# The norms' reciprocal square roots in a Flamingo-style stack on one core: a power on GpSimd in place of Newton rounds on VectorE

## What is computed

```python
def _layernorm(x, axis=-1, eps=1e-05):
    m = jnp.mean(x, axis=axis, keepdims=True)
    v = jnp.var(x, axis=axis, keepdims=True)
    return (x - m) / jnp.sqrt(v + eps)

x = x + jnp.tanh(g_xattn[0]) * _L0_xattn_ref(_layernorm(x), ctx, ...)   # differential attention
x = x + jnp.tanh(g_ffn[0])   * _L0_ffn_ref(_layernorm(x), ...)          # three coupled rotations
x = x + jnp.tanh(g_xattn[1]) * _L1_xattn_ref(ctx, _layernorm(x), mask, ...)
x = x + jnp.tanh(g_ffn[1])   * _L1_ffn_ref(_layernorm(x), ...)          # 2 shared + 8 routed experts
x = x + jnp.tanh(g_xattn[2]) * _L2_xattn_ref(_layernorm(x), ctx, ctx, ...)
x = x + jnp.tanh(g_ffn[2])   * _L2_ffn_ref(_layernorm(x), ...)          # attention, then 8 experts
x = x + jnp.tanh(g_xattn[3]) * _L3_xattn_ref(_layernorm(x), ctx, ctx, ...)
x = x + jnp.tanh(g_ffn[3])   * _L3_ffn_ref(_layernorm(x), ...)
```

```python
def layernorm(x, g, b):
    mu = jnp.mean(x, axis=-1, keepdims=True)
    var = jnp.var(x, axis=-1, keepdims=True)
    return (x - mu) * jax.lax.rsqrt(var + EPS) * g + b
```

## Time and profile before

| What | Value |
|---|---|
| Runs | 5879.70, 5902.63, 5884.03 us |
| Median | 5884.03 us |
| Span of the profiled execution | 5884.8 us |
| TensorE busy | 4971.8 us, 84% |
| VectorE busy | 3010.4 us, 51% |
| ScalarE busy | 1835.7 us, 31% |
| POOL busy | 404.4 us, 7% |
| Mean granted TensorE clock | 0.908 |

### The profile page before, as it was taken

The page is one execution under the profiler, slowest core; times in us unless marked ns, Lnnn a source line. Parts: engine busy times, 40 slices in busy tenths (PEclk is TensorE's granted clock), DMA queues, the critical chain, the costliest instruction groups (busy, mean ns, idle before and its releaser), DMA issues.

```text
span 5884.8 us, 74338 instructions
## 1 busy us (share of the span) xinstructions
PE 4971.8 (84%) x29184; PEld 3568.6 (61%) x29184; DVE 3010.4 (51%) x7402; ACT 1835.7 (31%) x3060; POOL 404.4 (7%) x244
## 2 busy tenths in 40 slices
PE   6998789987899878998789887798877988789887
PEld 4565755657556575565755657556675566655666
DVE  5445554455444555445554555535555355553555
ACT  3324143241432414224142241422424224142231
POOL 0000200001000020001100011000110001100011
PEclk8998889988799888998889999899998999989898
DMA  2000100001000010000100001000000000000000
GB/s 92 1 28 8 36 25 1 28 8 36 25 1 28 6 38 25 1 28 8 36 25 1 28 8 36 25 1 28 15 29 25 1 28 15 33 22 1 28 15 33
DMA packets 34483, 126.67 MB, mean 22 GB/s; under 512 B 3136, under 2 KB 15424, under 8 KB 25664
## 3 DMA queue, kind: packets, MB, share of 16 engines
q1 hardware_dynamic: 34112, 121.62, 6.0%
HBM read 117.41 MB, written 4.19 MB: 21 GB/s over the span
## 4 chain that ended last, share of the span: by engine, by line
PE 65%; DVE 24%; ACT 5%; issue 4%; DMA 1%; SPq 0%; POOL 0%; DVEq 0%; ACTq 0%
PE w L409 15%; PE w L419 9%; DVE mx L1006 7%; PE o L550 6%; PE w L666 5%; DVE oth_lo L1294 5%; PE w L508 4%; PE w L522 4%; PE w L399 4%; PE w L658 4%; PE o L543 4%; PE w L475 2%; ACT oth L769 2%; PE w L525 1%; DVE ob_hi L1293 1%
## 5 line engine op out<-in xcount | busy, mean ns | idle before, releaser
L807 ACT ACTIVATE pt<-w 128x1024 f32<-128x1024 f32 x640 | 653.3, 1023 | 765.4 <-PE w L525 440.5
L1006 DVE TENSOR_REDUCE mx<-w 128x4 f32<-128x1024 f32 x512 | 592.9, 1219 | 169.3 <-PE w L458 150.0
L769 ACT ACTIVATE oth<-w,res 128x256 f32<-128x256 f32 x656 | 263.6, 474 | 1036.5 <-PE w L658 905.2
L550 PE MATMUL o<-pt,va 128*32 128x256 f32 x4096 | 554.1, 407 | 18.5 <-ACT pt L807 18.5
L1236 DVE TENSOR_REDUCE mx<-w 128x2 f32<-128x1024 f32 x128 | 156.9, 1226 | 526.8 <-PE w L510 526.8
L666 PE MATMUL w<-ksp,ob_hi 128*128 128x256 f32 x1024 | 211.3, 339 | 251.2 <-DVE oth_lo L1294 251.2
L409 PE MATMUL w<-xnT,res 128*128 128x256 f32 x1408 | 371.6, 415 | 33.8 <-ACT xnT L761 24.5
L1367 POOL TENSOR_TENSOR stream_lo<-stream,ksp 128x2048 fp32r<-128x2048 f32 x64 | 309.0, 4828 | 852.5 <-DVE ksp L1289 852.5
L1294 DVE TENSOR_TENSOR oth_lo<-oth,ob_hi 128x1024 fp32r<-128x1024 f32 x128 | 359.2, 2806 | 4.4
L976 DVE SCALAR_TENSOR_TENSOR x<-w,gate,x 128x256 f32<-128x256 f32 x512 | 223.6, 478 | 258.0 <-PE w L666 235.7
L658 PE MATMUL w<-qsp,ksp 128*128 128x256 f32 x2048 | 353.1, 290 | 0.0
(11 more groups left out here) (235 smaller groups left out, 7955.5 us busy)
## 6 DMA issues: line engine op xcount, KB each, us to landing
stream<-in_moe_dram SPq DMA_DIRECT2D x64, 1024.0 KB, 4.8
stream<-in_moe_dram SPq DMA_DIRECT2D x80, 384.0 KB, 4.3
res<-in_resident_dram SPq DMA_DIRECT2D x1, 8157.5 KB, 22.2
cx<-in_ctx_dram SPq DMA_DIRECT2D x16, 256.0 KB, 3.6
x<-in_x_dram SPq DMA_DIRECT2D x16, 256.0 KB
out_dram<-x SPq DMA_DIRECT2D x16, 256.0 KB, 2.3
stream<-in_stage_dram SPq DMA_DIRECT2D x1, 2048.0 KB, 26.6
mrow<-in_mask_dram SPq DMA_DIRECT2D x16, 0.2 KB
```

The lines of the kernel that those rows point to most:

```text
L550: mm = pe.matmul(o[g:g + 32, 0:T], by_heads(plan, s)[:, kt, plan.v_of(h), :], pt[:, n % EXPS, a * 512 + kt * T:a * 512 + (kt + 1) * T], st ...
L769: h = act.activation(dst[:, c, :], w[:, c * T:(c + 1) * T], func, bias=bias[:, c:c + 1], **more)
L807: act.activation(pt[:, n % EXPS, :], w[:, :], ACT.Exp, scale=scale).then_inc(S["s_P"], 1)
L1006: dve.tensor_reduce(mx[s][:, :, 2 * u:2 * u + 2].rearrange("p t a -> p a t"), w[:, :].rearrange("p (a t k) -> p a t k", a=2, t=TT), AX_X, ...
```

## The change

- The function `rsqrt`, the copies and sums of the doubled norm, and the constant for the first guess go away. The scratch tile `nt` becomes `power`, filled with -0.5.
- `normalise` takes the statistics, raises `s_var`, waits for `s_rstd` and writes the normalised tile. Between the two, POOL's new `rstd` adds the epsilon and raises to the power -0.5, two instructions on two columns.
- For `l1.ln` the two norms in a row become one expression, the root of `var * (1 + eps) + eps * eps`, in one tensor_scalar ahead of the same power.
- In `l0.norm` VectorE raises `s_var` after it has scaled the sums and goes on. POOL makes the power on 32 columns itself, and then its two products.
- POOL's part of each norm stands at the norm's place in the list. There are two semaphores more and one less.

```diff
-            def rsqrt(v, y):
-
-                t = nt[:, 0:v.shape[-1]]
-                link(dve.tensor_scalar(y.bitcast(I32), v.bitcast(I32), -0.5, RSQRT_MAGIC, ALU.mult, ALU.add))
-                for _ in range(3):
-                    link(dve.scalar_tensor_tensor(t, y, -0.5, y, ALU.mult, ALU.mult))
-                    link(dve.tensor_tensor(t, t, v, ALU.mult))
-                    link(dve.scalar_tensor_tensor(y, t, 1.5, y, ALU.add, ALU.mult))
-
-            def normalise(dst, src, twice=False):
-
-                v, r = ve[:, 0:TT], rs[:, 0:TT]
-                link(stats_of(lambda tt: src[:, tt, :], mv))
-                link(dve.tensor_scalar(v, mv[:, :, 1], EPS, None, ALU.add))
-                rsqrt(v, r)
-                if twice:
-
-                    once = rc[:, 0:TT]
-                    link(dve.tensor_copy(once, r))
-                    link(dve.tensor_tensor(v, once, once, ALU.mult))
-                    link(dve.tensor_tensor(v, v, mv[:, :, 1], ALU.mult))
-                    link(dve.tensor_scalar(v, v, EPS, None, ALU.add))
-                    rsqrt(v, r)
-                    link(dve.tensor_tensor(r, r, once, ALU.mult))
+            def normalise(dst, src, step, s):
+
+                stats_of(lambda tt: src[:, tt, :], mv).then_inc(S["s_var"], 1)
+                dve.wait_ge(*after("s_rstd", step, s))
                 for tt in range(TT):
-                    h = dve.tensor_scalar(dst[:, tt, :], src[:, tt, :], mv[:, tt, 0:1], r[:, tt:tt + 1], ALU.subtract, ALU.mult)
+                    h = dve.tensor_scalar(dst[:, tt, :], src[:, tt, :], mv[:, tt, 0:1], rs[:, tt:tt + 1], ALU.subtract, ALU.mult)
                 return h
...
-            dve.memset(nt[:, :], 0.0)
+            dve.memset(power[:, :], -0.5)
...
-                        link(dve.tensor_scalar(ve[:, :], ve[:, :], 1.0 / 16, EPS, ALU.mult, ALU.add))
-                        rsqrt(ve[:, :], rs[:, :])
-                        signal(dve.tensor_copy(rms[s][:, :], rs[:, :]), "s_ms", step, s)
+                        dve.tensor_scalar(ve[:, :], ve[:, :], 1.0 / 16, EPS, ALU.mult, ALU.add).then_inc(S["s_var"], 1)
...
+            def rstd(step, s):
+
+                pool.wait_ge(*after("s_var", step, s))
+                var, r = mv[:, :, 1], rs[:, 0:TT]
+                if step == "l1.ln":
+                    link(pool.tensor_scalar(r, var, 1.0 + EPS, EPS * EPS, ALU.mult, ALU.add))
+                else:
+                    link(pool.tensor_scalar(r, var, EPS, None, ALU.add))
+                pool.tensor_tensor(r, r, power[:, 0:TT], ALU.pow).then_inc(S["s_rstd"], 1)
...
+                    elif what in ("ln", "cln") or step == "l1.out":
+                        rstd(step, s)
                     elif step == "l0.norm":
 
                         o = ob[s][:, 0:512].rearrange("p (n d) -> p n d", d=16)
-                        pool.wait_ge(*after("s_ms", step, s))
+                        pool.wait_ge(*after("s_var", step, s))
+                        signal(pool.tensor_tensor(rms[s][:, :], ve[:, :], power[:, :], ALU.pow), "s_rstd", step, s)
                         link(pool.tensor_tensor(o, o, rms[s][:, :].unsqueeze(2).to_broadcast([P, 32, 16]), ALU.mult))
                         pool.tensor_tensor(o, o, subw[:, :].unsqueeze(1).to_broadcast([P, 32, 16]), ALU.mult).then_inc(S["s_o"], 1)
```

More of the change, by code:

```diff
@@ L26 @@
 EXPS = 2
-RSQRT_MAGIC = float(0x5F3759DF)
 MASKED = 3.0e38
@@ L272, in build @@
         rs = sb("rs", [P, 32])
-        nt = sb("nt", [P, 32])
+        power = sb("power", [P, 32])
         rc = sb("rc", [P, 32])
@@ L1093, in out1 @@
                 y = tmp[:, :].rearrange("p (t c) -> p t c", t=TT)
-                h = normalise(y, w[:, 0:TT * D].rearrange("p (t c) -> p t c", t=TT))
+                h = normalise(y, w[:, 0:TT * D].rearrange("p (t c) -> p t c", t=TT), "l1.out", s)
                 signal(h, "s_xadd", "l1.out", s)
@@ L1202, in _ @@
                             dve.tensor_scalar(maskb[s][:, :], mrow[s][:, :], 1.0, MASKED, ALU.subtract, ALU.mult)
-                        signal(normalise(xt[s], x[s], stage == "l1"), "s_xt", step, s)
+                        signal(normalise(xt[s], x[s], step, s), "s_xt", step, s)
                     elif step in ("l2.v", "f2.v") or stage in ("l0", "l2", "f2") and what in ("k", "q", "max", "shift"):
@@ L1232, in _ @@
                         full(dve, "l0.exp", s, L0.units - 1)
-                        signal(normalise(qz[s], cx[s]), "s_xt", step, s)
+                        signal(normalise(qz[s], cx[s], step, s), "s_xt", step, s)
                     elif step == "l1.max":
@@ L1334, in link, with signal @@
                 pool.wait_ge(S["s_pool"], chain[0])
+            def signal(ins, name, step, s, u=0):
+                ins.then_inc(S[name], 1)
+                pool.wait_ge(*after(name, step, s, u))
+            def rstd(step, s):
[6 more added lines that the diff above has]
+                pool.tensor_tensor(r, r, power[:, 0:TT], ALU.pow).then_inc(S["s_rstd"], 1)
             def zeros_and_ones(st, s):
```

## The result

The changed kernel is slower by 0.6%: a median of 5929.23 us over four runs (5921.57 to 5931.13) beside 5886.1 us for the kernel before (four runs, 5879.7 to 5902.63), ratio 1.006 with a 95% interval of 1.0042 to 1.0077. The forecast was 5836 us, the range ended at 5888.

What follows compares the result with a forecast made beforehand. TensorE, busy 84%, bounds the kernel; VectorE savings count only where TensorE waits. Gains of 6.28 less 0.1 and 0.06 make 6.1 us a pass, 49 us off 5884.8: 5836 us, range 5808 to 5888.

Steps and rivals of the forecast that it cites:

- the price of the power on 32 columns: POOL's power in `l0.norm`, absent from the trace: bounded by a 0.17 us memset and 4.8 us work, taken as 2.5 us.
- 0.1 us a pass lost in slot 0: At `l0.norm`, slot 0: POOL's products start 2.66 us after the scaled sums instead of 2.55, costing 0.1 us a pass.
- Rival 1: Power costs 0.15 us a column, 4.9 us on 32; 2.3 us a pass of gain left, 5866 us; chance 0.25.
- Rival 2: Slower: power at 0.25 us a column, 8.1 us on 32, loses 4.5 us a pass, 5921 us; chance 0.09.
- rival 4: Shorter stop at `l1.out` keeps TensorE's clock up: 2.4 us a pass, 19 us, giving 5817 us; chance 0.10.
- The narrow norms: Two-column layer norms: power 0.25 us, round trip to POOL 0.72 us, so each norm's 2.20 us gap shrinks by 1.48.
- Five stops for `xt`: TensorE's five shorter waits for normalised tiles, each below 1.48 us, go whole: 3.02 us a pass.
- that of `l1.out`: Slot 1: TensorE's 5.42 us wait for the `f1.up` product, queued behind this norm on VectorE, shrinks by 1.48 us.
- The 0.3 us at `l2.ln` of slot 1: This norm stands ahead of maxima for which TensorE waits 0.27 us; gain taken as 0.3 us a pass.
- The 12 norms at nothing: Remaining 12 of 20 norms a pass gain nothing: their transposes come later in TensorE's queue than the data.
- Rival 3: The MODIFY_POOL_CONFIG pair is long at a pass's start, giving back 1.8 us a pass, 5850 us; chance 0.08.
- Rival 5: POOL round trip is as long as the Newton rounds, 2.2 us, so nothing is shortened: 5885 us; chance 0.05.

Runs made afterwards that it cites:

- its two shifted forms: The changed kernel with 8 or 24 extra SyncE clears of an unused semaphore at each pass's end: 5908.64 us and 5910.6 us.
- the second: The kernel before with only the 32-column root of `l0.norm` as a power on POOL, layer norms still by Newton rounds: 5954.61 us against 5889.9, ratio 1.0111.
- fourth experiments: The changed kernel with a product in place of the two-column power in the 160 layer norms, 32-column power kept: 5928.69 us against 5889.9, ratio 1.0072.
- the first: The changed kernel with the 32-column root of `l0.norm` back on VectorE as Newton rounds: 5856.25 us against 5889.9, ratio 0.9945.
- the sixth experiment: The kernel before with only the doubled norm `l1.ln` as one expression, still Newton rounds on VectorE: 5890.89 us against 5889.63, ratio 1.0.

## Why the prediction was wrong

- **The failed step** is the price of the power on 32 columns: "I take the middle, 2.5 us", between 0.17 and 4.8 us. It measured 5.43 us, above the upper end. That end was the longest thing POOL did in the trace, but a bound by other operations isn't a bound on this one: the experiment with the product shows a factor of 20 between two operations of the same instruction. The step "0.1 us a pass lost in slot 0" became 3.04 us there and 1.75 in slot 1. The experiments show it as the cause of the slowdown: without the wide power the change gains 33.7 us, the wide power alone loses 64.7, and with a product in its place the time is 109 us lower.
- **Rival 1** named the mechanism, with its price: at 0.15 us a column it gives 4.9 us for 32 columns. The measured slope of 0.157 is almost that. But it left out the 0.4 us fixed, and its time of 5866 us has no clock in it. Rival 2, the slower side, asked for 0.24 us a column, and that isn't what happened either: the kernel became slower at 0.157, where the prediction's own sum still gives a gain.
- **What the sum would be with measured prices.** Gains: 1.06 + 3.02 + 1.06 + 0.06 = 5.20, and 0.86 for the stop at the rotations that nobody had counted; losses: 3.04 + 1.75 + 0.06 = 4.85; 1.2 us a pass faster, some 5875 us. The stops in the trace say the same (9.4 us less in all). So even with every duration known the sum would have missed 5929 by some 54 us.
- **The second missing term** is the clock, which the prediction put at nothing outside rival 4: it counts what a stop lasts, and not that the same matmuls can take longer around it. They took 64.6 us longer after the change, and the wide power alone cost 64.7 us for 39.3 us of stops. How much of this the length of the stop brings and how much the place of the passes in time stays open. The traces show both at work: in the traces with the wide power (the changed kernel, its two shifted forms, and the second and fourth experiments) the clock behind the 4.6 us was never above 0.82, and behind 1.5 us (the kernel before, with and without clears, the first and the sixth experiment) it was anything from 0.63 to 1.00.
- **The narrow norms** were right in their places, though not in their price: the power on two columns took 0.71 us, for 0.25 forecast and 0.40 as its upper end. Five stops for `xt` went whole, 3.02 us a pass, as said. The last is shorter by 1.1 us, and so is that of `l1.out` (4.34 us for 5.42), because the round trip is 1.14 us and not 0.72. The 0.3 us at `l2.ln` of slot 1 didn't come: a stop of 0.21 us is still there for 0.27. The gain of the narrow part, 5.2 us a pass, is 42 us in all, and the two versions that have it without the wide power measured 33.7 and 42.9 (the second with 1.7 us of shorter stops for `ob` in it). That the second comes so near is in part luck: in its trace TensorE's idle time fell by 57.5 us against the kernel before, and its busy time rose by 20.1.
- **The 12 norms at nothing** were right: no new stop for `xt` came with the change, and the doubled one has an experiment of its own. VectorE's busy time fell by 356 us (355 said).
- **Rival 3**, the configuration pair, is false. It moved to the pass's start as said, one pair a pass, sixteen instructions in all:

```profile
L1327 POOLq MODIFY_POOL_CONFIG  x16: 11/11/11, 33.8 to 5188.7; - x16
```

  In later passes POOL starts 0.09 us after VectorE's aggregates (2245.40 to 2245.49). In the first pass the pair stands at 33.8 us and the first tensor_scalar starts at 37.5, so that what follows the pair takes at most 3.7 us there. The Trainium skill, "GPSIMD Engine Reference", section 2.1, gives about 6 us for the first call after code has been loaded; this trace has room for less than that in the first pass.
- **Rival 4**, a clock kept up at `l1.out`, is false: the matmuls behind the shorter stop still take the 2.05 us of the earlier trace rows:

```profile
2586.18 2.05 PE L420 MATMUL w<-stream,oth 128*128 128x256 f32 x4 [4.34 <-DVE oth L1232]
```

  Its idea, that the clock moves the time beside the stops, was right and in the wrong place: the clock fell behind `l0.norm`, from 0.63 to 0.88 before the change to 0.60 to 0.82 after it, and mostly to the lower end.
- **Rival 5**, a round trip as long as the Newton rounds, is false: 1.14 us for 2.20.

## What to carry to other kernels

Before a function is moved to another engine, ask for its price by the element at the widest tile on which it is called: here one change held two cases, 2 columns where the power is a gain and 32 where it costs more than twice the rounds that it replaces, and only the split of the two is worth having. A bound from other operations on the same engine is no bound; where the trace has no row for an operation, give the expensive side of the range more than the nearest rows suggest, above all where the result is already awaited. And when a change makes a stop of TensorE longer, look at its busy time for the same matmuls as well as at the stop, and do so in every pass: one pass set beside one pass could have shown here a clock of 0.63 against 0.82, or of 0.88 against 0.61.

## What the runs showed of the hardware

- A power on POOL takes 713 ns on two columns and 5427 on 32, where a product of the same tiles takes 197 and 253: some 157 ns a column by these two points, against 2 for the product.
- A signal from VectorE to POOL took 0.09 us, one between two POOL instructions 0.08, and one from POOL back to VectorE 0.04, so that the hand-over itself is cheap: 0.21 us a round trip.
- The same pass, with the same counts on every engine, takes 728.6 or 737.6 us in one execution, at granted clocks of 0.91 and 0.89. Eight more semaphore clears by SyncE at each pass's end moved the changed kernel by 0.3%, and two other kernels not measurably. A difference of that size between two kernels of this kind isn't yet a difference between their instructions.
- Behind one and the same stop of 1.54 us TensorE's mean granted clock over 14 us was 0.63, 0.76 or 0.88 in the passes of one execution, and behind 4.6 us 0.61 or 0.82. With no stop there, in the product's run, it was 1.00 in all eight passes, and behind 1.33 us as well.
- Shorter stops needn't shorten the time: with the product in place of the narrow power, 7.3 us fewer of them came with 13.1 us more of TensorE's busy time, and the same total.
